# A recurrent attention kernel whose banks for projections, gate inputs and output quarters are dealt out anew, with VectorE's additions in another order

## The chip, the cores and the metric

The kernel runs on one core of one Trainium2 chip. The metric is the device time of one execution in microseconds (us). TensorE (PE) multiplies, VectorE (DVE) and ScalarE (ACT) read and write the accumulator memory PSUM and the on-chip memory SBUF, GpSimd (POOL) works on SBUF alone, and SyncE (SP) issues the DMAs. Every engine works through a list of its own in order, and the engines wait for each other through semaphores. PSUM has eight banks here, numbered 0 to 7; each holds 512 fp32 values in each of the 128 partitions.

## The reference, cut to what matters

For an input of 4 batches, 512 tokens and 256 features:

```python
xn = layernorm(x)
s  = attention(xn)               # below, 16 key heads, two value heads for each
g  = silu(feed_forward(xn))      # weights are looked up in a table of 16 values
out = x + s * g

# attention, for each head
q, k, v = silu(causal_conv(xn @ W_qkv, 4 taps))
z = xn @ W_z
T = inverse(I + strictly_lower(beta * k @ k.T * decay))      # chunks of 64 tokens
v_c, k_cumdecay = T @ (v * beta), T @ (k * beta * exp(g))
for each chunk:                                              # 8 chunks, in sequence
    v_new = v_c - k_cumdecay @ state
    o     = (q * exp(g)) @ state + (q @ k.T * decay) @ v_new
    state = state * exp(g_last) + (k * exp(g_last - g)).T @ v_new
s += (norm_w * rmsnorm(o) * silu(z)) @ W_out
```

## The kernel before

The work is done in 32 rounds. A round is one key head (`R.h`) with two of the four batches (`R.par`), and holds two value heads of 512 tokens in 8 chunks. A round has three stages, and each engine's part of them is written out by hand:

- `begin`: products of keys with keys and queries, and transposes. VectorE then inverts the 16x16 diagonal blocks alone (`small_blocks`, ends with L1175) while TensorE projects the first half of the **next** round's q, k, v (`proj` 0 to 3) and adds the **previous** round's output quarters 0 and 1 (`outputs`, kind `out`, L680).
- `invert`: two levels (16 to 32, 32 to 64) complete the inverse. A level is `products` first (L482, L484, banks 2 and 3), ScalarE's copy (`first_products`, L872), `products` second (L487, L489), and VectorE's predicated copy into the inverse (`second_products`, L1200). Between these TensorE does what the tables at the top of the program name for each place (`beside`): the rest of the projections (`PROJ_AT`, L425), output quarters of the previous round (`OUT_AT`), and inputs of the gate (`Z_AT`, `zproj`, L452). VectorE fills its time with the convolution of the next round's projections: for each of four kinds (key, query, two values) ScalarE makes tap 0 (`tap0`, L772), VectorE adds taps 1 to 3 out of the banks (`taps`, L1024), ScalarE applies silu (`silu`, L780). VectorE also scales the previous round's last quarter of the attention (`gated` 3, L1285), out of the bank into which TensorE has turned it (`turn_back` 3, kind `ot3`, L667), and adds the four output quarters (128 tokens of two batches each) to the sum `acc` (L1294).
- `keys_through` (L580: the keys go through the inverse; kind `kcd`, four groups in banks 4, 5, 6, 7, two for each batch), ScalarE's copies of them (L918), and then `recur`, the chain over the 8 chunks. It opens with half of the last gate input (z3), and `old_part` (L588), which needs banks 4 and 5 empty again; VectorE's L1245 follows it.

Order on ScalarE behind the second level: silu of value 0, gate 0, silu of value 1 (`silu` 3, waits for the last of all the taps), gates 1 and 2 (`gate`, L812, each reads one z bank), the copies of `kcd`, gate 3.

What ties the work together is `bank_uses`: a list for each round of (use, bank). Every use of a bank waits until the one before it in the same bank has been read. `wait_open` and `wait_full` look the numbers up, `full[n]` counts what TensorE has filled in bank n and `read[n]` what has been read from it. `keys_through` waits for both banks of a batch before its first product. `both` names the PSUM tensor that starts at an even bank, because a kind's two batches are read as one pair of banks.

Of the kernel before, what the change touches and what calls it, by code (L numbers as in the profile page):

```python
# [42 lines left out]
IN_LEVELS = 3  # L43
OUT_LAST = {(5, 1): (3,)}
PROJ_FIRST = (0, 1, 2, 3)
PROJ_AT = {(4, 1): (4, 5), (5, 1): (6, 7)}
OUT_AT = {(4, 0): (1,), (5, 0): (2,), (5, 1): (3,)}
Z_AT = {(5, 1): (0, 1, 2)}
GATE_UP_AT = {(4, 0): ((0, 0),), (4, 1): ((0, 1),), (5, 0): ((1, 0), (1, 1)), (5, 1): ((2, 0), (2, 1))}
PROJ = [("proj", i) for i in range(8)]  # L50
# [7 lines left out]
def bank_uses(it):  # L58

    first, nxt = it == 0, it < ROUNDS - 1  # L60
    begin = (spread([("kkq", i) for i in range(2)], (4, 5)) + spread([("kt", i) for i in range(2)], (6, 7))
             + spread([("vt", i) for i in range(4)], (1, 4, 5, 7)))
    ahead = spread(PROJ, (0, 1, 6, 7)) if nxt else []
    outs = [] if first else spread([("out", 0), ("out", 1), ("out", 2), ("ot3", 0), ("out", 3)], (5, 4, 5, 4, 4) if nxt else (5, 4, 7, 4, 5))
    levels = []
    for lv in LEVELS:
        levels += spread([("p1", (lv, b)) for b in range(BB)], (2, 3)) + spread([("p2", (lv, b)) for b in range(BB)], (2, 3))
    small = spread([("z", i) for i in range(4)], (5, 0, 1, 0) if nxt else (0, 1, 0, 0)) + (spread(N2, (0, 1)) if nxt else [])
    keys = spread([("kcd", i) for i in range(4)], (4, 5, 6, 7))
    steps = spread([("vn", n) for n in range(NC * BB)], (4, 5)) + spread([("sp", c) for c in range(NC - 1)], (6,))  # L70
    turns = spread([("o", i) for i in range(4)], (2, 3)) + spread([("ot", i) for i in range(3 if nxt else 4)], (1,))
    end = [] if nxt else spread([("end", i) for i in range(4)], (0, 2))
    return begin + outs + ahead + levels + small + keys + steps + turns + end


def all_places():
# [61 lines left out]
def build(nc, x, consts, resets_in, wqkvz, wba, convw, dtb, alog, normw, wout, lut, idx, out):  # L138
    g_dram = nc.dram_tensor("g_scratch", (B, HV, S), F32, kind="Internal").ap()
    fw_dram = nc.dram_tensor("fw_scratch", (HQK, 2, P, SLICE), F32, kind="Internal").ap()  # L140
    with ExitStack() as ctx:
# [78 lines left out]
        ps_p2 = ctx.enter_context(nc.psum_tensor("ps_p2", [P, BB, 512], F32))  # L220
        ps_state = ctx.enter_context(nc.psum_tensor("ps_state", [P, RATIO, 512], F32))
        ps = [t[:, n, :] for t in (ps_two, ps_p1, ps_p2, ps_state) for n in range(2)]
        both = {0: ps_two, 6: ps_state}
        G = ps_p1[:, 0, 0:BASE * (BASE + 1)]
        full = [sem(f"full{i}") for i in range(8)]
        read = [sem(f"read{i}") for i in range(8)]
# [154 lines left out]
        def _(pe):  # L381
# [134 lines left out]
            def invert(R):  # L516

                if R.nxt:
                    for i in PROJ_FIRST:
                        proj(R, i)  # L520
                if R.before() is not None:
                    for t in range(1 if R.nxt else 3):
                        outputs(R, "out", R.before(), t)
                    if R.nxt:
                        outputs(R, "out", R.before(), 1, (0,))
                for n, lv in enumerate(LEVELS):
                    pe.wait_ge(s["xs"], R.at(1 + 2 * n, 0, 4))
# [15 lines left out]

            def beside(R, lv, half):

                if R.before() is not None and (lv, half) == (5, 1):
                    turn_back(R.before(), 3)
                if R.nxt:
                    for i in PROJ_AT.get((lv, half), ()):
                        proj(R, i)  # L550
                else:
                    for f, j in GATE_UP_AT[lv, half]:
                        if f == 0 and j == 0:
                            pe.wait_ge(s["ld_fw"], 16)
                        if f == 1 and j == 0:
                            wait_read(pe, R, "out", 2)
                        if f >= 2 and j == 0:
                            pe.wait_ge(s["ff_h"], f - 1)
                        gate_up(f, f, 0, j, AHEAD[f])
                if R.before() is not None:  # L560
                    for t in (OUT_AT if R.nxt else OUT_LAST).get((lv, half), ()):
                        outputs(R, "out", R.before(), t, (1,) if t == 1 else (0, 1))
# [181 lines left out]
        def _(act):  # L744
# [94 lines left out]
            def invert(R):  # L839
                if R.nxt:  # L840
                    tap0(R, 0)
                if R.nxt:
                    tap0(R, 1)
                small_x(R)
                swap(R, 0)
                first_products(R, 4)
                if R.nxt:
                    silu(R, 0)
                swap(R, 1)
                if R.nxt:  # L850
                    tap0(R, 2)
                else:
                    gated_unit(0, 0, AHEAD[0])
                first_products(R, 5)
                if R.nxt:
                    silu(R, 1)
# [94 lines left out]
        def _(dve):  # L951
# [249 lines left out]

            def invert(R):
                of = R.before()
                if R.nxt:
                    taps(R, 0, (1, 2, 3))
                if of is not None:
                    for t in range(1 if R.nxt else 3):
                        outputs(R, "out", of, t)
                second_products(R, 4, 2)
                turn()  # L1210
                if R.nxt:
                    taps(R, 1, (1, 2, 3))
                else:
                    hidden(0, 0, AHEAD[0])
                    hidden(1, 1, AHEAD[1])
                if R.nxt and of is not None:
                    outputs(R, "out", of, 1)
                second_products(R, 5, 4)
                if of is not None:
                    gated(of, 3)  # L1220
                if R.nxt and of is not None:
                    outputs(R, "out", of, 2)
                if R.nxt:
                    taps(R, 2, (1, 2, 3))
                else:
                    hidden(2, 2, AHEAD[2])
                if of is not None:
                    outputs(R, "out", of, 3)
                if R.nxt:
                    taps(R, 3, (1, 2, 3))  # L1230

            def second_products(R, lv, n):

# [278 lines left out]
```

## Time and profile before

| what | us |
|---|---|
| median of 3 runs (2178.72 to 2179.42) | 2178.77 |
| the profiled execution | 2178.21 |
| its span, first to last instruction | 2176.4 |
| from one round to the next in mid-run | 61.3 |
| TensorE busy | 2070.3 |
| GpSimd busy | 1670.5 |
| VectorE busy | 1597.4 |
| ScalarE busy | 1192.7 |

Busy shares are means over stages that differ. For this change only the middle of a round is needed: from the end of `small_blocks` to the first chunk of `recur`. The timeline of each engine shows it: an instruction's start, its length, and in square brackets how long the engine had stood idle before it and who released it.

### The profile page before, as it was taken

How to read it: one execution, taken by the hardware profiler on the slowest of the kernel's cores; microseconds unless marked ns; L12 is line 12 of the kernel's file. 1: busy time of each engine (PE TensorE's matmuls, PEld its weight loads, DVE VectorE, ACT ScalarE, POOL GpSimd, SP SyncE). 2: the span in 40 equal slices, each digit the busy share in tenths (PEclk: the TensorE clock that was granted, in tenths of full speed). 3: DMA queues.
4: the chain of work that ended last, by engine and by line, in shares of the span. 5: the costliest groups of instructions: out<-in, count | busy, mean ns of one | idle time of the engine just before them, and what ended most of it. 6: DMA issues, size and time to landing. Idle time of an engine off the chain costs nothing.

```text
span 2176.4 us, 75165 instructions
## 1 busy us (share of the span) xinstructions
PE 2070.3 (95%) x31952; PEld 1578.1 (73%) x31952; DVE 1597.4 (73%) x3083; ACT 1192.7 (55%) x2757; POOL 1670.5 (77%) x1774
## 2 busy tenths in 40 slices
PE   3799999999999999999999999999999999999998
PEld 2677777777777777777777777777777777776644
DVE  5777777778777777778777777778777777776322
ACT  3565556655665556655665556655665556654211
POOL 2788888888888888888888888888888888888200
PEclk9899999999999999999999999999999999999999
DMA  2211101111121101121121102111121102111100
GB/s 87 58 41 39 48 17 41 39 48 34 36 48 39 47 16 44 39 49 34 36 48 39 47 14 46 39 48 34 36 48 39 48 11 48 39 39 45 45 15 20
DMA packets 57485, 86.31 MB, mean 40 GB/s; under 512 B 7488, under 2 KB 30144, under 8 KB 57152
## 3 DMA queue, kind: packets, MB, share of 16 engines
q1 hardware_dynamic: 57152, 81.50, 15.2%
q8 instruction: 254, 4.16, 0.8%
q14 instruction: 79, 0.65, 0.1%
HBM read 76.92 MB, written 4.55 MB: 37 GB/s over the span
## 4 chain that ended last, share of the span: by engine, by line
PE 49%; DVE 33%; ACT 9%; issue 6%; POOL 2%; DMA 0%; DVEq 0%; POOLq 0%; SPq 0%; ACTq 0%
DVE cacc L1024 11%; PE ps_two L452 8%; PE ps_state L425 5%; PE ps_p L615 4%; DVE terms L1126 3%; PE ps_p L501 3%; ACT qg L799 3%; PE ps_state L639 3%; PE ps_p L680 3%; PE ps_p L623 3%; PE ps_p L588 3%; PE ps_p L452 2%; PE ps_p L739 2%; ACT L790 2%; PE ps_two L539 2%
## 5 line engine op out<-in xcount | busy, mean ns | idle before, releaser
L1411 POOL TENSOR_SCALAR Kg<-idx_s,lutb 128x134 f32<-128x134 int32 x480 | 356.3, 745 | 27.1
L1372 POOL TENSOR_TENSOR Sd<-St,el 128x512 f32<-128x512 f32 x192 | 201.3, 1048 | 196.9 <-DVEq L1266 196.9
L1245 DVE TENSOR_SCALAR Vn<-ps_p,bR 128x128 f32<-128x128 f32 x512 | 165.9, 349 | 189.8 <-PE ps_p L588 114.1
L425 PE MATMUL ps_two<-xnT,w_qkv 128*128 128x256 f32 x1024 | 235.7, 383 | 17.7 <-DVEq L1029 17.7
L1024 DVE SCALAR_TENSOR_TENSOR cacc<-ps_state,cw,cacc 128x1022 f32<-128x1022 f32 (+2 forms) x192 | 244.2, 1272 | 7.9 <-ACT cacc L772 3.1
L1024 DVE SCALAR_TENSOR_TENSOR cacc<-ps_two,cw,cacc 128x1022 f32<-128x1022 f32 (+2 forms) x192 | 244.8, 1275 | 5.3 <-DVE cacc L1024 0.5
L680 PE MATMUL ps_p<-w_o,hT 128*128 128x256 f32 x1000 | 242.4, 386 | 1.6 <-ACT V L835 1.6
L425 PE MATMUL ps_state<-xnT,w_qkv 128*128 128x256 f32 x1024 | 234.0, 382 | 5.9 <-DVEq L1029 5.9
L425 PEld LDWEIGHTS ps_two<-xnT,w_qkv 128*128 128x128 f32 x1024 | 190.3, 191 | 44.3 <-DVEq L1029 21.0
L425 PEld LDWEIGHTS ps_state<-xnT,w_qkv 128*128 128x128 f32 x1024 | 193.7, 192 | 32.3 <-DVEq L1029 6.3
L927 ACT ACTIVATE P<-ps_p 128x128 f32<-128x128 f32 x256 | 67.2, 277 | 267.7 <-PE ps_p L593 267.7
L680 PEld LDWEIGHTS ps_p<-w_o,hT 128*128 128x128 f32 x1000 | 185.2, 190 | 27.6 <-issue 2.8
L1264 DVE TENSOR_TENSOR St<-Sd,ps_state 128x256 f32<-128x256 f32 x384 | 144.4, 417 | 68.8 <-PE ps_state L639 39.0
L452 PE MATMUL ps_two<-xnT,w_z 128*128 128x512 f32 x388 | 188.9, 610 | 0.2
L1383 POOL TENSOR_TENSOR qg<-qg,kq 128x512 f32<-128x512 f32 x128 | 166.5, 1324 | 17.6 <-DVE blocks L1097 17.6
L615 PE MATMUL ps_p<-St,Kg 128*64 128x128 f32 x1792 | 163.3, 294 | 6.3 <-DVE St L1264 6.1
L588 PE MATMUL ps_p<-V,XW 64*64 64x128 f32 x2048 | 159.6, 271 | 0.0
L593 PE MATMUL ps_p<-Vn,A 64*64 64x128 f32 x2048 | 155.9, 270 | 3.5
L1417 POOL TENSOR_TENSOR Kg<-Kg 128x536 f32<-128x536 f32 (+2 forms) x128 | 142.4, 1112 | 10.2
L639 PE MATMUL ps_state<-Vn,Kd 64*64 64x128 f32 x3584 | 149.6, 282 | 0.1
L772 ACT ACTIVATE cacc<-ps_state,cw 128x1024 f32<-128x1024 f32 x64 | 71.2, 1113 | 135.9 <-PE ps_state L425 101.0
L588 PEld LDWEIGHTS ps_p<-V,XW 64*64 64x64 f32 x2048 | 120.9, 133 | 24.7 <-ACT Kg L918 23.5
(192 smaller groups left out, 5014.4 us busy)
## 6 DMA issues: line engine op xcount, KB each, us to landing
qg<-g_scratch SPq DMA_DIRECT2D x64, 512.0 KB, 6.2
g_st<-g_scratch SPq DMA_DIRECT2D x64, 256.0 KB, 8.6
w_qkv<-in_wqkvz SPq DMA_DIRECT2D x16, 512.0 KB, 3.8
w_z<-in_wqkvz SPq DMA_DIRECT2D x16, 256.0 KB, 3.3
w_o<-in_wout SPq DMA_DIRECT2D x16, 256.0 KB, 2.9
idx_s<-in_idx SPq DMA_DIRECT2D x32, 67.0 KB, 1.9
fw_scratch<-looked_up SPq DMA_DIRECT2D x32, 67.0 KB, 2.7
Kg<-in_x SPq DMA_DIRECT2D x2, 1024.0 KB, 5.7
```

What stands on the lines that cost most here:

```text
L425: m = pe.matmul(bank[:, t0:t0 + S // 2], w_qkv[:, k, kind * P:(kind + 1) * P], rows, start=(k == 0), stop=(k == KD - 1))
L452: m = pe.matmul(bank[:, :], w_z[:, k, a * P:(a + 1) * P], xnT[:, k, cols(R.par, b)], start=(k == 0), stop=(k == KD - 1))
L588: return pe.matmul(bank[r, 0:P], X[r, b, c, :], V[r, b, c, :], start=True, stop=(c == 0), skip_group_check=True)
L593: return pe.matmul(o_bank[turned[a], o0:o0 + P], A[r, b, c, :], Vn[r, c % 2, b, :], start=(c == 0 and b == 0), stop=True, skip_group_check ...
L615: m = pe.matmul(olds[b][0][r, 0:P], Kg[:, b, c, r], St[:, cur, a, b, :], start=False, stop=True, skip_group_check=True)
L639: m = pe.matmul(ps[6 + a][half, b * P:(b + 1) * P], Kd[r, b, c, half], Vn[r, cur, b, :], start=True, stop=True)
L680: m = pe.matmul(bank[:, b * D:(b + 1) * D], hT[:, t, a, 1 - b, :], w_o[:, a, :], start=(a == 0), stop=(a == RATIO - 1))
L1024: dve.scalar_tensor_tensor(dst, both[n][:, :, 0:S - t], cw[:, kind, 3 - t:4 - t], dst, ALU.mult, ALU.add).then_inc(s["taps"], 1)
L1245: dve.tensor_scalar(Vn[:, cur, b], bank[:, 0:P], bR[:, R.par, b, c:c + 1], None, ALU.mult).then_inc(done, 1)
L1372: pool.tensor_tensor(Sd[:, :, :, :], St[:, c % 2, :, :, :], el[:, R.par, :, :, c].unsqueeze(3).broadcast_to([P, BB, RATIO, P]), ALU.mult). ...
L1383: m = pool.tensor_tensor(dst, dst, kq[:, :, 1, b, :], ALU.mult)
L1411: m = pool.tensor_scalar(slots[k], idx_s[:, :], float(k), lutb[:, k:k + 1], ALU.is_equal, ALU.mult)
```

## The change

The table of banks and the two orders (TensorE's and VectorE's) are rewritten for the rounds that have a next one (31 of 32; the last round keeps its order and banks). In words:

- Banks. The next round's projections 4 to 7 move from banks 0, 1, 6, 7 to 4, 5, 0, 1. Output quarter 2 moves from bank 5 to 6, the turned quarter `ot3` and output quarter 3 from bank 4 to 7. The gate inputs z0, z1, z2 move from 5, 0, 1 to 4, 5, 2.
- TensorE. Output quarter 1 stands whole behind the first products of level 4; half of it stood ahead of them. Output quarter 2 leaves its place between the products of level 5; projection 6 takes it. At the end of the levels comes projection 7, then `ot3`, then quarters 2 and 3.
- VectorE. Output 0 is added ahead of the first tap of kind 0, output 1 behind this tap; tap 1 of kind 2 goes ahead of `gated` 3, and taps 2 and 3 behind it; then outputs 2 and 3 together, then the taps of kind 3.
- ScalarE. Tap 0 of kind 2 goes behind the copy of level 5's first products; it stood ahead.

```diff
-PROJ_AT = {(4, 1): (4, 5), (5, 1): (6, 7)}
-OUT_AT = {(4, 0): (1,), (5, 0): (2,), (5, 1): (3,)}
+PROJ_AT = {(4, 1): (4, 5), (5, 0): (6,), (5, 1): (7,)}
+OUT_AT = {(4, 0): (1,), (5, 1): (2, 3)}
...
-    ahead = spread(PROJ, (0, 1, 6, 7)) if nxt else []
+    ahead = spread(PROJ, (0, 1, 6, 7, 4, 5, 0, 1)) if nxt else []
...
-    small = spread([("z", i) for i in range(4)], (5, 0, 1, 0) if nxt else (0, 1, 0, 0)) + (spread(N2, (0, 1)) if nxt else [])
+    small = spread([("z", i) for i in range(4)], (4, 5, 2, 0) if nxt else (0, 1, 0, 0)) + (spread(N2, (0, 1)) if nxt else [])
...
-                    if R.nxt:
-                        outputs(R, "out", R.before(), 1, (0,))
```

TensorE, end of the levels up to `recur`, in a round of mid-run (`ps_p2` is banks 4 and 5, `ps_state` 6 and 7, `ps_two` 0 and 1, `ps_p1` 2 and 3; `waits read5` is the wait until bank 5 has been read). Before:

```order
L452 MATMUL ps_p2<-xnT,w_z 128x512 [waits read5,ld_wz]
L452 MATMUL ps_p2<-xnT,w_z 128x512
L452 MATMUL ps_two<-xnT,w_z 128x512 [waits read0]
L452 MATMUL ps_two<-xnT,w_z 128x512
L452 MATMUL ps_two<-xnT,w_z 128x512 [waits read1]
L452 MATMUL ps_two<-xnT,w_z 128x512
L580 MATMUL ps_p2<-XW,Kg 64x64 [waits read4,read5,kg_c,xs]
L580 MATMUL ps_p2<-XW,Kg 64x64 x31
L580 MATMUL ps_state<-XW,Kg 64x64 [waits read6,read7,kg_c,xs]
```

The same place now:

```order
L453 MATMUL ps_p2<-xnT,w_z 128x512 [waits read4,ld_wz]
L453 MATMUL ps_p2<-xnT,w_z 128x512
L453 MATMUL ps_p2<-xnT,w_z 128x512 [waits read5]
L453 MATMUL ps_p2<-xnT,w_z 128x512
L453 MATMUL ps_p1<-xnT,w_z 128x512 [waits read2]
L453 MATMUL ps_p1<-xnT,w_z 128x512
L582 MATMUL ps_p2<-XW,Kg 64x64 [waits read4,read5,kg_c,xs]
L582 MATMUL ps_p2<-XW,Kg 64x64 x31
L582 MATMUL ps_state<-XW,Kg 64x64 [waits read6,read7,kg_c,xs]
```

The second gate input (z1) stood in bank 0 and stands in bank 5 now, the bank that the key products behind it write.

VectorE, from the end of `small_blocks` (XW) through the first level. Before:

```order
L1175 TENSOR_SCALAR XW<-terms,cst 128x16x16
L1024 SCALAR_TENSOR_TENSOR cacc<-ps_two,cw,cacc 128x2x511 [waits tap0]
L1024 SCALAR_TENSOR_TENSOR cacc<-ps_two,cw,cacc 128x2x510 [waits taps]
L1024 SCALAR_TENSOR_TENSOR cacc<-ps_two,cw,cacc 128x2x509 [waits taps]
L1294 TENSOR_TENSOR acc<-acc,ps_p2 128x2x256 [waits taps,full5]
L1198 MEMSET carry 128x1 [waits full3,full2]
L1200 COPY_PREDICATED XW<-cst,ps_p1 128x32x16
```

Now (`waits full4` is the wait until TensorE has filled bank 4):

```order
L1176 TENSOR_SCALAR XW<-terms,cst 128x16x16
L1298 TENSOR_TENSOR acc<-acc,ps_p2 128x2x256 [waits full5]
L1025 SCALAR_TENSOR_TENSOR cacc<-ps_two,cw,cacc 128x2x511 [waits tap0]
L1298 TENSOR_TENSOR acc<-acc,ps_p2 128x2x256 [waits full4]
L1025 SCALAR_TENSOR_TENSOR cacc<-ps_two,cw,cacc 128x2x510 [waits taps]
L1025 SCALAR_TENSOR_TENSOR cacc<-ps_two,cw,cacc 128x2x509 [waits taps]
L1199 MEMSET carry 128x1 [waits taps,full3,full2]
L1201 COPY_PREDICATED XW<-cst,ps_p1 128x32x16
```

Output 1 stands behind the first tap, and what follows it on the engine waits with it.

TensorE around the first level, with the 32x32 and 64x32 products of the level left out. Before:

```order
L680 MATMUL ps_p2<-w_o,hT 128x256 [waits read4,normed_o]
L680 MATMUL ps_p2<-w_o,hT 128x256
...
L680 MATMUL ps_p2<-w_o,hT 128x256 x2
...
L425 MATMUL ps_two<-xnT,w_qkv 128x256 [waits read0]
L425 MATMUL ps_two<-xnT,w_qkv 128x256 x3
L425 MATMUL ps_two<-xnT,w_qkv 128x256 [waits read1]
L425 MATMUL ps_two<-xnT,w_qkv 128x256 x3
```

Now:

```order
L682 MATMUL ps_p2<-w_o,hT 128x256 [waits read4,normed_o]
L682 MATMUL ps_p2<-w_o,hT 128x256 x3
...
L426 MATMUL ps_p2<-xnT,w_qkv 128x256 [waits read4]
L426 MATMUL ps_p2<-xnT,w_qkv 128x256 x3
L426 MATMUL ps_p2<-xnT,w_qkv 128x256 [waits read5]
L426 MATMUL ps_p2<-xnT,w_qkv 128x256 x3
```

Two matmuls of quarter 1 stood ahead of the first products and two behind; all four stand behind now. Projection 4 waited for bank 0, and waits for bank 4.

## Rows read from the trace of the kernel before

**Rows 1.** The page: busy time of the engines, and the chain that ended last.

```profile
PE 2070.3 (95%) x31952; PEld 1578.1 (73%) x31952; DVE 1597.4 (73%) x3083; ACT 1192.7 (55%) x2757; POOL 1670.5 (77%) x1774
PE 49%; DVE 33%; ACT 9%; issue 6%; POOL 2%; DMA 0%; DVEq 0%; POOLq 0%; SPq 0%; ACTq 0%
```

**Rows 2.** Timeline of VectorE, one round: start us, length us, engine, line, operation.

```profile
887.62 0.65 DVE L1175 TENSOR_SCALAR XW<-terms,cst 128x256 f32<-128x256 f32 x2
888.19 3.89 DVE L1024 SCALAR_TENSOR_TENSOR cacc<-ps_two,cw,cacc 128x1022 f32<-128x1022 f32 x3
892.32 0.69 DVE L1294 TENSOR_TENSOR acc<-acc,ps_p 128x512 f32<-128x512 f32 x1 [0.25 <-DVE cacc L1024]
892.93 0.74 DVE L1200 COPY_PREDICATED XW<-cst,ps_p 128x512 f32<-128x512 int32 x1
...
893.91 0.71 DVE L1190 STREAM_TRANSPOSE XW<-XW 128x512 f32<-128x512 f32 x1 [0.24 <-DVE XW L1200]
894.55 3.87 DVE L1024 SCALAR_TENSOR_TENSOR cacc<-ps_state,cw,cacc 128x1022 f32<-128x1022 f32 x3
...
900.36 0.75 DVE L1285 SCALAR_TENSOR_TENSOR hT<-ps_p,gpar,z 128x512 f32<-128x512 f32 x1 [0.24 <-PE ps_p L667]
901.26 0.69 DVE L1294 TENSOR_TENSOR acc<-acc,ps_p 128x512 f32<-128x512 f32 x1
...
906.62 3.90 DVE L1024 SCALAR_TENSOR_TENSOR cacc<-ps_state,cw,cacc 128x1022 f32<-128x1022 f32 x3
913.97 0.61 DVE L1245 TENSOR_SCALAR Vn<-ps_p,bR 128x128 f32<-128x128 f32 x2 [3.45 <-PE ps_p L588]
...
948.89 0.65 DVE L1175 TENSOR_SCALAR XW<-terms,cst 128x256 f32<-128x256 f32 x2
```

**Rows 3.** Timeline of TensorE in the same round.

```profile
885.40 2.75 PE L680 MATMUL ps_p<-w_o,hT 128*128 128x256 f32 x12
888.32 0.24 PE L482 MATMUL ps_p<-XW,U 64*64 64x32 f32 x1 [0.17 <-DVE XW L1175]
...
889.38 1.13 PE L680 MATMUL ps_p<-w_o,hT 128*128 128x256 f32 x4
...
892.19 3.72 PE L425 MATMUL ps_two<-xnT,w_qkv 128*128 128x256 f32 x16 [0.59 <-DVEq L1029]
...
896.52 1.99 PE L680 MATMUL ps_p<-w_o,hT 128*128 128x256 f32 x8
...
899.50 0.63 PE L667 MATMUL ps_p<-cst,on 128*128 128x128 f32 x4 [0.30 <-DVE acc L1294]
...
906.86 3.60 PE L452 MATMUL ps_two<-xnT,w_z 128*128 128x512 f32 x8
910.39 1.16 PE L580 MATMUL ps_p<-XW,Kg 64*64 64x64 f32 x64
...
912.43 1.12 PE L452 MATMUL ps_two<-xnT,w_z 128*128 128x512 f32 x2
913.48 0.66 PE L588 MATMUL ps_p<-V,XW 64*64 64x128 f32 x8
```

**Rows 4.** Timeline of ScalarE in the same round.

```profile
892.11 1.06 ACT L780 ACTIVATE kq<-cacc 128x1024 f32<-128x1024 f32 x1 [1.91 <-DVE cacc L1024]
...
910.55 1.06 ACT L780 ACTIVATE vs<-cacc 128x1024 f32<-128x1024 f32 x1 [2.89 <-DVE cacc L1024]
911.52 1.06 ACT L812 ACTIVATE z<-ps_two 128x512 f32<-128x512 f32 x2
912.47 1.08 ACT L918 ACTIVATE Kg<-ps_p 128x512 f32<-128x512 f32 x2
```

**Rows 5.** Waits of the whole run: engine and line, releaser, us in total, times, longest.

```profile
PEld ps_p L588 <- ACT Kg L918: 23.5, 31, 0.8
```

**Rows 6.** Timeline of TensorE in the first round.

```profile
92.31 0.31 PE L482 MATMUL ps_p<-XW,U 64*64 64x32 f32 x1 [3.57 <-DVE XW L1175]
```

**Rows 7.** Window of it: length, busy PE, PEld, DVE, ACT, POOL, then PEclk.

```profile
92.30:94.30 2.00, 1.93 (x64) 1.80 (x64) 1.96 (x2) 1.17 (x2) 1.77 (x4) 0.50 0.04 8
```

More of the change, by code:

```diff
@@ L62, in bank_uses @@
              + spread([("vt", i) for i in range(4)], (1, 4, 5, 7)))
-    ahead = spread(PROJ, (0, 1, 6, 7)) if nxt else []
-    outs = [] if first else spread([("out", 0), ("out", 1), ("out", 2), ("ot3", 0), ("out", 3)], (5, 4, 5, 4, 4) if nxt else (5, 4, 7, 4, 5))
+    ahead = spread(PROJ, (0, 1, 6, 7, 4, 5, 0, 1)) if nxt else []
+    outs = [] if first else spread([("out", 0), ("out", 1)], (5, 4))
+    late = [] if first else spread([("out", 2), ("ot3", 0), ("out", 3)], (6, 7, 7) if nxt else (7, 4, 5))
     levels = []
@@ L72, in bank_uses @@
     end = [] if nxt else spread([("end", i) for i in range(4)], (0, 2))
-    return begin + outs + ahead + levels + small + keys + steps + turns + end
+    return begin + outs + ahead + late + levels + small + keys + steps + turns + end
 def all_places():
@@ L222, in build @@
         ps = [t[:, n, :] for t in (ps_two, ps_p1, ps_p2, ps_state) for n in range(2)]
-        both = {0: ps_two, 6: ps_state}
+        both = {0: ps_two, 4: ps_p2, 6: ps_state}
         G = ps_p1[:, 0, 0:BASE * (BASE + 1)]
@@ L544, in beside @@
             def beside(R, lv, half):
-                if R.before() is not None and (lv, half) == (5, 1):
+                turn = R.before() is not None and (lv, half) == (5, 1)
+                if turn and not R.nxt:
                     turn_back(R.before(), 3)
@@ L550, in beside @@
                         proj(R, i)
+                    if turn:
+                        turn_back(R.before(), 3)
                 else:
@@ L561, in beside @@
                     for t in (OUT_AT if R.nxt else OUT_LAST).get((lv, half), ()):
-                        outputs(R, "out", R.before(), t, (1,) if t == 1 else (0, 1))
+                        outputs(R, "out", R.before(), t)
                 for i in Z_AT.get((lv, half), ()):
@@ L849, in invert @@
                 swap(R, 1)
-                if R.nxt:
-                    tap0(R, 2)
-                else:
+                if not R.nxt:
                     gated_unit(0, 0, AHEAD[0])
@@ L855, in invert @@
                 if R.nxt:
+                    tap0(R, 2)
                     silu(R, 1)
@@ L1203, in invert @@
                 of = R.before()
-                if R.nxt:
-                    taps(R, 0, (1, 2, 3))
-                if of is not None:
-                    for t in range(1 if R.nxt else 3):
-                        outputs(R, "out", of, t)
+                if not R.nxt:
+                    for t in range(3):
+                        outputs(R, "out", of, t)
+                    second_products(R, 4, 2)
+                    turn()
+                    hidden(0, 0, AHEAD[0])
+                    hidden(1, 1, AHEAD[1])
+                    second_products(R, 5, 4)
+                    gated(of, 3)
+                    hidden(2, 2, AHEAD[2])
+                    outputs(R, "out", of, 3)
+                    return
+                if of is not None:
+                    outputs(R, "out", of, 0)
+                taps(R, 0, (1,))
+                if of is not None:
+                    outputs(R, "out", of, 1)
+                taps(R, 0, (2, 3))
                 second_products(R, 4, 2)
                 turn()
[L1211 to L1217, printed above, removed]
+                taps(R, 1, (1, 2, 3))
                 second_products(R, 5, 4)
+                taps(R, 2, (1,))
                 if of is not None:
                     gated(of, 3)
-                if R.nxt and of is not None:
+                taps(R, 2, (2, 3))
+                if of is not None:
                     outputs(R, "out", of, 2)
[L1223 to L1227, printed above, removed]
                     outputs(R, "out", of, 3)
-                if R.nxt:
-                    taps(R, 3, (1, 2, 3))
+                taps(R, 3, (1, 2, 3))
             def second_products(R, lv, n):
```

## The prediction

> **What bounds the kernel now.** I read the chain of waits first, then the timelines of the three engines over one round of mid-run, and last the table of waits. The page names TensorE, 95% busy, and a chain that is half TensorE and a third VectorE [rows 1]: in some stretch of each round VectorE is what comes last. Rounds follow each other every 61.27 us (L1175 at 887.62 and at 948.89 [rows 2]), and their rows repeat within some hundredths, so one round, times 31, is the sum.
>
> The round's middle begins when VectorE ends the small inverse (L1175, 887.62 + 0.65 = 888.27). TensorE starts the first products at 888.32, behind an idle time of 0.17 only [rows 3]. VectorE then has no gap above 0.25 us until its last tap ends at 906.62 + 3.90 = 910.52 [rows 2]. TensorE is just as full: one stop of 0.59 before projection 4 (banks 0 and 1, which the taps of kind 0 read), one of 0.30 before the turned quarter, and then no gap through the gate inputs, the key products (L580, 910.39) and half of z3, up to `old_part` (L588, 913.48) [rows 3]. ScalarE joins at the end: silu of the last value at 910.55, 0.03 behind the last tap, gates 1 and 2 at 911.52, the first two key copies at 912.47, ended at 913.55 [rows 4]. `old_part` starts together with their end, and the weight loads of L588 waited for the copies in 31 rounds, 0.76 us each [rows 5]. So two chains meet at 913.5: TensorE's own queue, and VectorE's last tap, silu, gates, copies. Nothing shortens a round there unless both get shorter, and either can lengthen it alone. VectorE's first V_new (L1245, 913.97) follows.
>
> **The change part by part.** Before the end of the small inverse TensorE loses half an output quarter, 12 records of L680 becoming 8. It was waiting there for VectorE anyhow (0.17), and the first products still wait for L1175: worth nothing.
>
> *Term A, VectorE's wait for output 1.* VectorE now does output 0 (start to start 892.93 - 892.32 = 0.61) and one tap (3.89 / 3 = 1.30) from 888.19 on, and would be ready for output 1 at 888.19 + 0.61 + 1.30 = 890.10. TensorE reaches the quarter only behind the first products, at 889.38, and a whole quarter takes 1.99 (L680 x8), not the 1.13 of a half [rows 3]: it ends at 891.37, and I put VectorE's start at 891.44, a release later. That is 1.34 us of idle time on a full engine. The additions and taps are otherwise the same instructions, and their 0.24 and 0.25 stops behind a tap or a predicated copy are as many as before; one start-to-start distance shrinks by about 0.1 because an output no longer stands ahead of the second predicated copy. Followed through by these lengths: taps of kind 0 end at 894.65 (before 892.08), the second products of level 4 are long there, the turn starts 895.87 (before 893.91), taps of kind 1 end 900.40, and the last tap of kind 3 ends at 911.77. **A = 911.77 - 910.52 = 1.25 us** a round.
>
> What else VectorE needs on this way should be there in time. The second products of level 5 stand behind projection 6 now (half of 3.72), so TensorE ends them at about 899.9; VectorE asks at 900.6. The turned quarter stands behind projection 7 and ends at about 902.3; VectorE asks at 902.9. ScalarE's silu of the key moves with the taps from 892.11 to 894.67, and its copy of level 5's first products ends near 898.7, under projection 6, which covers TensorE until 899.2. These covers are 0.5 to 0.7 us thick; if one fails, VectorE ends by that much later.
>
> *Term B, the key products wait for gate 1.* z1 is in bank 5 now, and the key products of batch 0 wait for banks 4 and 5 before their first matmul. Bank 5 is read by gate 1, and gate 1 stands on ScalarE behind the silu that waits for the last tap. Before, gate 1 started 911.52 - 910.52 = 1.00 behind the last tap, and one of the two takes about 0.59 (two in 1.06) [rows 4]. With 0.06 for the release TensorE can start 1.65 behind the last tap. Before it started 0.13 **ahead** of it (910.39 against 910.52 [rows 3]), because bank 5 held z0, whose gate runs much earlier, and bank 4 output 3. **B = 1.65 + 0.13 = 1.78 us.** Behind the waiting product stand all the key products, z3 and `old_part`, with nothing in between that could be pulled ahead. VectorE is idle by then (3.45 before L1245), and ScalarE has only gate 2 to do: no work hides the wait.
>
> *Term C, what TensorE gets back.* Banks 6 and 7 are empty earlier (output 2 and 3 instead of projections 6 and 7), but TensorE gets to them behind the products that wait. The 0.59 and 0.30 stops go, and the time is spent in front of the later wait: the gate inputs, started about 906.5 when the taps of kind 2 have left bank 4, end at about 911.7, 1.7 us before gate 1 is through. Behind the key products the two halves of the end chain no longer meet: the copies have 2.04 us of key products and half of z3 to run under. The distance from L580 to L588 was 3.09 (910.39 to 913.48); half of z3 alone is 0.88 of it by the pace of the other gate inputs (3.60 for four matmuls less a tail), against the 1.05 it stood for. **C = -0.15 us.**
>
> Sum of a round: 1.25 + 1.78 - 0.15 = 2.88 us. The first round has no previous outputs, but has the same gate 1 in bank 5, and the last has no next round and keeps its order; with 31 rounds the sum is 31 x 2.88 = 89 us. The profiled execution, 2178.21 (span 2176.4 and 1.8 around it), becomes 2267.5; the median of the runs is 0.56 above the profiled one: 2268, and I round the unknown release times up to **2269 us**.
>
> The bounds: A is nothing at least, if VectorE takes up the wait elsewhere, and at most 1.34 + 0.7 with one failed cover. B lies between 1.6 (the gate's start and length, no release) and 1.9. C lies between 0 and -0.76, the whole wait of L588's weights for the copies [rows 5]. A round costs 0.8 to 3.9 with all ends on one side, and 2.3 to 3.5 where they are not: 2250 to 2287.
>
> A page speaks for this change. The Trainium skill, Perfetto Trace Analysis, section Optimizing Tensor Performance, says that independent matmul groups should rotate through different banks, so that one group's evacuation overlaps the next group's matmuls. By that alone the key products gain, since two of their four banks come free earlier; it gives the second rival below. The trace agrees on the evacuations (TensorE runs on through z0 to z2 while gate 0 reads), but what decides here is which instruction empties the bank and what stands ahead of it on its engine.
>
> **The rivals.** *Only B.* VectorE's wait for output 1 costs nothing in the end, since the last tap also waits for things that come at their old time. The round costs 1.78 - 0.15 = 1.63, 31 of them 51 us: 2229. Against it: VectorE's rows show no slack between L1175 and the last tap that could take 1.3 us up.
>
> *TensorE's queue decides: faster.* If the key products find bank 5 empty when TensorE comes to them, as now, because gate 1 does get ahead of the last tap, TensorE's queue alone counts. It saves the stops of 0.59 and 0.30 and pays 1.99 - 1.13 = 0.86 for the half quarter that stood under a wait: together -0.03, and up to -0.15 more at z3. 31 rounds give -1 to -6 us, 2173 to 2178. It decides if the gate is through by 910.4; for it speaks that TensorE is the fuller engine of the page [rows 1], against it that ScalarE works in order, that the order puts gate 1 behind the silu of the last value, and that this silu began 0.03 behind the last tap [rows 4].
>
> *The change does not do what it says*: moved work fills the same waits and the round stays within 0.1 us. It would need both of the above to cancel: 2175 to 2182.
>
> *The clock falls.* TensorE's stop before the key products grows to some 1.7 us in every round. In the first round it stood for 3.57 us before the first products [rows 6], and these ran at a granted clock of 0.50, its 1.2 GHz level, and took 1.93 for the 64 matmuls [rows 7] that take 889.38 - 888.32 = 1.06 in mid-run: 1.8 times as long. If 1.7 us were enough, the 2.9 us from the key products to `old_part` would take 2.3 more, 71 us in all: 2340. The trace has stops of 0.59 in every round at the full clock and none of 1.7, so it does not exclude this. The Trainium skill, TensorE: Matmul & The Clock Gate, says that the gate follows how busy TensorE has recently been; the first round agrees, and whether 1.7 us is enough no row shows.
>
> **How the numbers follow.** Forecast (A, B and C as above) 0.80, 2269, its own bounds 2250 to 2287. Only B 0.10, 2229. One cover failed and more, 0.03, up to 2300. Clock 0.02, 2340. TensorE's queue decides 0.03, 2176. No change 0.02. The range 2250 to 2287 holds the first and leaves out the rest. A measurement of this kernel tells about 0.2% (4.4 us) from no change: faster by more 0.02, within 0.03, slower by more 0.95.
>
> **What would show it.** In the profile after: idle time of 1.2 to 1.4 us before VectorE's first L1298 output 1, released by TensorE's L682 (A); 31 stops of about 1.7 us before L582, released by ScalarE's gate L814, and the weight loads of L590 no longer waiting for the copies (B, C); the last tap ending some 23.5 us behind L1176 (22.25 before); rounds 64.1 us apart; PEclk at 1.00. The prediction is wrong if L582 starts before the last tap ends, if VectorE's last tap is not later than before, or if a cover fails and VectorE shows a new wait for full3 or full7.

## The result

| | before | after |
|---|---|---|
| median, us | 2179.10 (2178.72 to 2180.78, 4 runs) | 2302.64 (2300.26 to 2304.75, 4 runs) |
| the profiled execution, us | 2178.21 | 2302.11 |
| its span, us | 2176.4 | 2300.3 |
| an ordinary round, us | 61.26 | 64.40 |
| TensorE busy, us | 2070.3 | 2091.2 |
| VectorE busy, us | 1597.4 | 1591.7 |

The ratio is 1.0567, 95% interval 1.0551 to 1.0583. The sign and the two mechanisms of the forecast hold, and the time lies 16 us above the range, which ended at 2287.

The page of after, answering [rows 1], has TensorE's share of the last chain down from 49% to 36% and VectorE's up from 33% to 43%:

```profile
PE 2091.2 (91%) x31952; PEld 1578.3 (69%) x31952; DVE 1591.7 (69%) x3083; ACT 1194.9 (52%) x2757; POOL 1669.8 (73%) x1774
DVE 43%; PE 36%; ACT 11%; issue 7%; POOL 2%; DVEq 0%; DMA 0%; POOLq 0%; SPq 0%; ACTq 0%
```

VectorE in an ordinary round of after (start, length, engine, line, operation, then the idle time before it and who ended it), answering [rows 2]:

```profile
943.19 0.65 DVE L1176 TENSOR_SCALAR XW<-terms,cst 128x256 f32<-128x256 f32 x2
943.76 0.67 DVE L1298 TENSOR_TENSOR acc<-acc,ps_p 128x512 f32<-128x512 f32 x1
944.35 1.27 DVE L1025 SCALAR_TENSOR_TENSOR cacc<-ps_two,cw,cacc 128x1022 f32<-128x1022 f32 x1
946.99 0.69 DVE L1298 TENSOR_TENSOR acc<-acc,ps_p 128x512 f32<-128x512 f32 x1 [1.37 <-PE ps_p L682]
...
963.48 3.90 DVE L1025 SCALAR_TENSOR_TENSOR cacc<-ps_two,cw,cacc 128x1022 f32<-128x1022 f32 x3
972.68 0.61 DVE L1249 TENSOR_SCALAR Vn<-ps_p,bR 128x128 f32<-128x128 f32 x2 [5.29 <-PE ps_p L590]
```

The small inverse ends at 943.84. The last tap ends at 967.38, 23.54 later, and V_new starts at 28.84. In [rows 2] these distances were 910.52 - 888.27 = 22.25 and 913.97 - 888.27 = 25.70. VectorE waits 1.37 us for output 1 and 5.29 before V_new (3.45 before).

TensorE and ScalarE in the same round, answering [rows 3] and [rows 4]:

```profile
944.96 1.99 PE L682 MATMUL ps_p<-w_o,hT 128*128 128x256 f32 x8
...
962.24 5.39 PE L453 MATMUL ps_p<-xnT,w_z 128*128 128x512 f32 x12 [0.78 <-DVEq L1030]
969.11 1.16 PE L582 MATMUL ps_p<-XW,Kg 64*64 64x64 f32 x64 [1.48 <-ACT z L814]
970.06 1.15 PE L582 MATMUL ps_state<-XW,Kg 64*64 64x64 f32 x64
971.14 1.12 PE L453 MATMUL ps_two<-xnT,w_z 128*128 128x512 f32 x2
972.19 0.65 PE L590 MATMUL ps_p<-V,XW 64*64 64x128 f32 x8
```

```profile
967.42 1.06 ACT L782 ACTIVATE vs<-cacc 128x1024 f32<-128x1024 f32 x1 [2.59 <-DVE cacc L1025]
968.38 1.07 ACT L814 ACTIVATE z<-ps_p 128x512 f32<-128x512 f32 x2
```

The whole of output quarter 1 ends at 946.95, and VectorE takes output 1 at 946.99. The key products start at 969.11, 1.73 behind the last tap (25.27 behind the small inverse; 22.12 before), when the first of the two gates is through. `old_part` follows 3.08 later. Over the whole run (engine and line, releaser, us in total, times, longest):

```profile
DVE acc L1298 <- PE ps_p L682: 46.4, 33, 3.9
PE ps_p L582 <- ACT z L814: 44.7, 30, 1.8
PE ps_state L582 <- issue: 14.0, 8, 2.4
```

The third line has no counterpart before. An ordinary round is one of the length that most rounds share. Ordinary rounds are 64.40 apart, 3.14 longer, and 31 x 3.14 = 97.3 us. The other 26 us lie elsewhere. In ten rounds (counted from 0: 0, 5, 6, 10, 11, 16, 21, 22, 27, 28) TensorE stops once more in the middle of the key products or just behind them, 0.5 to 2.4 us, with "issue" as releaser: it waited for nothing that the profile shows. Round 11:

```profile
838.62 1.16 PE L582 MATMUL ps_p<-XW,Kg 64*64 64x64 f32 x64 [1.48 <-ACT z L814]
839.58 1.14 PE L582 MATMUL ps_state<-XW,Kg 64*64 64x64 f32 x60
842.06 0.33 PE L582 MATMUL ps_state<-XW,Kg 64*64 64x64 f32 x4 [1.35 <-issue]
```

The stops sum to 15.5 us. The nine such rounds behind round 0 are together 20.8 us longer than nine ordinary ones, partly because the clock also fell in rounds 5 and 10. Round 0 is 66.74 long (60.29 before), 3.3 beyond the 3.14; the last round is 1.4 longer. 97.3 + 20.8 + 3.3 + 1.4 = 122.8, of 123.9 between the spans.

### The profile page after: what moved, and what is told of

Read it like the earlier page. It is cut to its first block, busy times and chain, and to the rows that moved or that the text cites. A ratio compares the mean times of both kernels' runs of the same rounds, so it can differ in the third digit from the quotient of the medians.

```text
span 2300.3 us, 75165 instructions
## 1 busy us (share of the span) xinstructions
PE 2091.2 (91%) x31952; PEld 1578.3 (69%) x31952; DVE 1591.7 (69%) x3083; ACT 1194.9 (52%) x2757; POOL 1669.8 (73%) x1774
## 3 DMA queue, kind: packets, MB, share of 16 engines
q8 instruction: 254, 4.16, 0.8%
## 4 chain that ended last, share of the span: by engine, by line
DVE 43%; PE 36%; ACT 11%; issue 7%; POOL 2%; DVEq 0%; DMA 0%; POOLq 0%; SPq 0%; ACTq 0%
DVE cacc L1025 18%; PE ps_p L617 4%; PE ps_two L453 3%; DVE terms L1127 3%; PE ps_p L682 3%; PE ps_p L502 3%; ACT qg L801 3%; DVE acc L1298 3%; PE ps_state L641 3%; PE ps_p L590 2%; PE ps_p L625 2%; PE ps_p L741 2%; DVE XW L1201 2%; ACT L792 2%; PE ps_two L538 2%
## 5 line engine op out<-in xcount | busy, mean ns | idle before, releaser
L426 PE MATMUL ps_two<-xnT,w_qkv 128*128 128x256 f32 x1024 | 243.2, 385 | 0.0
L453 PE MATMUL ps_p<-xnT,w_z 128*128 128x512 f32 x372 | 170.0, 607 | 26.2 <-DVEq L1030 26.2
L590 PE MATMUL ps_p<-V,XW 64*64 64x128 f32 x2048 | 160.6, 272 | 1.5 <-issue 1.5
L782 ACT ACTIVATE vs<-cacc 128x1024 f32<-128x1024 f32 x64 | 67.5, 1057 | 166.5 <-DVE cacc L1025 166.5
L782 ACT ACTIVATE kq<-cacc 128x1024 f32<-128x1024 f32 x64 | 67.6, 1057 | 164.5 <-DVE cacc L1025 164.5
L453 PEld LDWEIGHTS ps_p<-xnT,w_z 128*128 128x128 f32 x372 | 69.2, 193 | 113.8 <-issue 113.8
L590 PEld LDWEIGHTS ps_p<-V,XW 64*64 64x64 f32 x2048 | 121.8, 134 | 26.5 <-issue 26.5
L1402 POOL TENSOR_TENSOR rr<-ss,cst 128x4 f32<-128x4 f32 x128 | 129.8, 1014 | 10.0
L625 PE MATMUL ps_p<-St,qg 128*64 128x128 f32 x1792 | 135.9, 273 | 0.0
L641 PEld LDWEIGHTS ps_state<-Vn,Kd 64*64 64x64 f32 x3584 | 95.5, 132 | 58.8 <-issue 36.0
```

The costliest lines, as they stand in the source:

```text
L426: m = pe.matmul(bank[:, t0:t0 + S // 2], w_qkv[:, k, kind * P:(kind + 1) * P], rows, start=(k == 0), stop=(k == KD - 1))
L453: m = pe.matmul(bank[:, :], w_z[:, k, a * P:(a + 1) * P], xnT[:, k, cols(R.par, b)], start=(k == 0), stop=(k == KD - 1))
L590: return pe.matmul(bank[r, 0:P], X[r, b, c, :], V[r, b, c, :], start=True, stop=(c == 0), skip_group_check=True)
L625: pe.matmul(o_bank[turned[a], o0:o0 + P], qg[:, R.par, a, b, c * C:(c + 1) * C], St[:, cur, a, b, :], start=(cur == 0 and b == 0), stop=False,
L641: m = pe.matmul(ps[6 + a][half, b * P:(b + 1) * P], Kd[r, b, c, half], Vn[r, cur, b, :], start=True, stop=True)
```

## The experiments

Four kernels take the two terms and the extra stops apart, and three more (e5, e6, e7) test what sets the pace of an ordinary round. Offsets below are from the end of the small inverse of that kernel, in ordinary rounds; that of the key products is their first weight load's, 0.03 ahead of the first matmul. Extra stops are TensorE's "issue" stops in or right behind the key products.

| kernel | median, us | last tap | key products | V_new | round | extra stops, us |
|---|---|---|---|---|---|---|
| before | 2179 | 22.25 | 22.11 | 25.69 | 61.26 | 0 |
| after | 2302.6 | 23.54 | 25.23 | 28.84 | 64.40 | 15.5 |
| e1 | 2234.1 | 23.54 | 23.71 | 27.29 | 62.88 | 0 |
| e2 | 2239.6 | 23.54 | 23.71 | 27.29 | 62.87 | 5.5 |
| e3 | 2262.5 | 22.26 | 23.95 | 27.55 | 63.12 | 17.1 |
| e4 | 2310.1 | 23.54 | 25.23 | 28.83 | 64.41 | 20.8 |
| e5 | 2206.8 | 22.68 | 22.84 | 26.44 | 62.01 | 0 |
| e6 | 2159.8 | 22.11 | 21.33 | 25.06 | 60.65 | 0 |
| e7 | 2178.9 | 22.26 | 22.11 | 25.70 | 61.28 | 0 |

**e1: the change with z1 out of bank 5.** Are the 1.5 us before the key products, and the extra stops with them, owed to bank 5?

```diff
-    small = spread([("z", i) for i in range(4)], (4, 5, 2, 0) if nxt else (0, 1, 0, 0)) + (spread(N2, (0, 1)) if nxt else [])
+    small = spread([("z", i) for i in range(4)], (4, 2, 3, 0) if nxt else (0, 1, 0, 0)) + (spread(N2, (0, 1)) if nxt else [])
```

> The changed kernel with one edit in the table of banks: the gate inputs z1 and z2 in banks 2 and 3 in place of 5 and 2, so that the key products no longer share a bank with z1. Theory (gate 1 holds bank 5 until behind the last tap, and TensorE, stopped in front of a dense run of small matmuls, runs out of fetched instructions in some rounds): the stop of 1.48 us before the key products goes, they start 23.8 us behind the small inverse (25.2 now), VectorE's first V_new stands at 27.1 (28.8 now, 25.7 before), no round has a stop of issue on TensorE in or behind the key products, and the time is 2178.8 + 31 x 1.4 = 2222 us, 2215 to 2232. Rival (VectorE's later last tap alone decides, the gate only fills time that is lost anyway): V_new stays at 28.8 or above 28.3 and the time stays above 2285.

Measured: 2234.09 (2230.84 to 2235.25), ratio 1.0252 (1.0236 to 1.0267). The time is 2 us above the range I gave. The last tap stays at 23.54, the wait for the gate is gone, and so are all extra stops:

```profile
931.51 5.39 PE L453 MATMUL ps_p<-xnT,w_z 128*128 128x512 f32 x12 [0.77 <-DVEq L1030]
936.83 1.16 PE L582 MATMUL ps_p<-XW,Kg 64*64 64x64 f32 x64
937.82 1.13 PE L582 MATMUL ps_state<-XW,Kg 64*64 64x64 f32 x64
```

The gate inputs now set the start of the key products. They wait for VectorE's taps of kind 2, which read bank 4, and end at 23.7. So z1's place in bank 5 costs 68.5 us of the 123 (z2 goes to bank 3 to make room): 31 x 1.52 = 47 by the ordinary rounds, the rest by what came with the wait. The remaining 1.6 a round belongs to the rest of the change: the two new orders and the other banks, z0's in bank 4 among them. e5 below takes 0.87 of it back.

**e2: the change with gate 1 ahead of the silu of value 1.** Bank and wait stay, and the releaser comes earlier.

```diff
+                    gate(R, 1)
                     silu(R, 3)
...
-                gate(R, 1)
```

> The changed kernel, all banks as it has them, with ScalarE's gate 1 moved ahead of the silu of the last value. The same question from the other side: bank 5 is emptied while VectorE is still in its last taps. Theory: as the kernel with z1 in bank 2, key products at 23.8 us, V_new at 27.1, no stops of issue, 2222 us (2215 to 2232). Rival: 2285 or more, since the silu stands 0.6 us further back on ScalarE only if the gate is not ready, and VectorE's end is unchanged.

Measured: 2239.57 (2238.29 to 2242.48), ratio 1.0277 (1.0260 to 1.0294). I had expected no extra stops and at most 2232. Ordinary rounds are those of e1, but rounds 0, 5, 10, 11, 16, 21, 22 and 27 stop again, shorter, 0.42 to 0.90 us. Round 10 of e2:

```profile
752.25 1.16 PE L582 MATMUL ps_p<-XW,Kg 64*64 64x64 f32 x64
753.23 0.77 PE L582 MATMUL ps_state<-XW,Kg 64*64 64x64 f32 x37
754.70 0.68 PE L582 MATMUL ps_state<-XW,Kg 64*64 64x64 f32 x27 [0.70 <-issue]
```

TensorE shows no wait before the products here, and yet the extra stop is there, of 0.70. What changed is when their wait is released: gate 1, at 750.64 and 0.60 long, ends 1.0 us ahead of them; in the change it ends 0.14 us ahead.

**e3: the kernel before with z1 in bank 5 alone.**

```diff
-    small = spread([("z", i) for i in range(4)], (5, 0, 1, 0) if nxt else (0, 1, 0, 0)) + (spread(N2, (0, 1)) if nxt else [])
+    small = spread([("z", i) for i in range(4)], (0, 5, 1, 0) if nxt else (0, 1, 0, 0)) + (spread(N2, (0, 1)) if nxt else [])
```

> The kernel before with one edit: z0 in bank 0 and z1 in bank 5 (they stood in 5 and 0). Nothing else of the change is in it. Theory: the key products wait for gate 1 as in the changed kernel and start 1.65 us behind the last tap (23.9 us behind the small inverse, 22.1 now), V_new at 27.3 (25.7 now), 31 x 1.6 = 50 us, and 15 to 25 us of instruction stops and slow clock in a third of the rounds on top: 2240 to 2255. Rival on the second half (the stops of issue come from another part of the change, the banks of the projections or the load of weights): V_new at 27.3 in every round, no stops of issue, 2226 to 2234. Rival on the first (the whole loss is in VectorE's order): 2178 to 2185.

Measured: 2262.49 (2261.82 to 2267.91), ratio 1.039 (1.0374 to 1.0405). z0 goes to bank 0 in exchange. Nothing else of the change is in it: the last tap stays at 22.26, and the round is 1.86 longer.

```profile
951.39 1.16 PE L580 MATMUL ps_p<-XW,Kg 64*64 64x64 f32 x64 [0.88 <-ACT z L812]
```

Its time is 7 us above the range I gave: a round costs 1.86 and not 1.6, which makes 58 us, and what comes on top is 25.5, at the upper end of the 15 to 25 I gave it. The extra stops come with the wait: 17.1 us in the same ten rounds. In round 10 it breaks off behind the same 37th matmul of the second half as the change and e2.

**e4: the change, shifted.** In the change, e2 and e3 round 10 breaks behind matmul 64 + 37. Count all of TensorE's instructions in the trace together, from 0: matmuls, weight loads, and its 1,105 semaphore and drain instructions, which the timeline leaves out. The key products of round 10 begin at a number that leaves 245 over 256. Behind 101 matmuls with their loads, and the two semaphore instructions between the two halves, the next is 245 + 2 x 101 + 2 = 449, which is 193 over 256. Round 11 begins at 199 and breaks behind 64 + 60 (199 + 2 x 124 + 2 = 449), round 0 at 193 behind 127 (449). In all 28 extra stops of the change, e2 and e3, those just behind the products too, the last instruction to go through stands 192 over a multiple of 256. Counted by matmuls and loads alone the stops share no such place. If it is a matter of place in the program, small repeated matmuls in the prologue must move it to other rounds (64 matmuls by the page, with their loads 128 instructions; they only repeat work).

```diff
+                    if R.head and i == 0:
+                        for _ in range(32):
+                            pe.matmul(bank[0:C, 0:WIDE], flat(sqk)[:, 0:C], ones[:, 0:WIDE], start=True, stop=True)
```

> The changed kernel with 32 more small matmuls in the prologue (each is repeated work, overwritten before it is read): 128 more records of TensorE ahead of every round, half of a block of 256 instructions in which they are fetched. Theory (a round stops when a block's border lies in the first 70 records behind the wait): the rounds with a stop of issue of 0.5 to 2.5 us, numbered from 0, are 5, 6, 10, 11, 16, 21, 22, 27, 28 in the changed kernel and become about 2, 7, 8, 13, 14, 19, 24, 25, 30; their number and the time stay, 2296 to 2310. Rival (the stops come with the weight load that SyncE issues behind the last tap of every second round, or with something else that has its place in the round's number): the stops stay in the same rounds. In every second round they cannot be, since 5, 11, 21, 27 and 6, 10, 16, 22 are both odd and even.

Measured: 2310.06 (2307.38 to 2312.98), ratio 1.0603 (1.0587 to 1.0619), at the upper end of the range. The extra stops are now in rounds 2, 7, 8, 13, 14, 18, 19, 24, 25 and 30. All ten stand behind number 192 over a multiple of 256 again. Nine of the rounds were named beforehand, from products that begin at 185 or more; round 18 was not: they begin at 5 there, and the border falls 187 instructions in. In the change's round 4 they begin at 9, the border falls 183 in, and there is no stop. Ordinary rounds are unchanged at 64.41. Round 2, whose products begin at 229 now, breaks behind matmul 64 + 45 (229 + 2 x 109 + 2 = 449):

```profile
246.75 1.16 PE L585 MATMUL ps_p<-XW,Kg 64*64 64x64 f32 x64 [1.48 <-ACT z L817]
247.70 0.90 PE L585 MATMUL ps_state<-XW,Kg 64*64 64x64 f32 x45
250.92 0.56 PE L585 MATMUL ps_state<-XW,Kg 64*64 64x64 f32 x19 [2.32 <-issue]
```

What lies behind it shows in the page's DMA queues. Two queues are of the kind "instruction". One of them, q8, moves 254 packets of 16 KB in the whole run, and TensorE has 65,009 instructions in the trace: one packet for every 256. The trace's view of the DMA in a short window (busy share in 40 slices, then the queue) finds the packet of round 11. In the kernel before, from 785.00 to 789.00, the products start at 787.86 and the packet stands in the 15th slice, at 786.4, 1.4 us ahead of them:

```profile
DMA  0000000000000070000000000000000000000000
q8 instruction: 1, 0.02, 1.9%
```

In the change, from 838.60 to 841.00 (products from 838.62), it stands in the 19th slice, at 839.7, 1.1 us **behind** their start:

```profile
DMA  0000000000000000009000000000000000000000
q8 instruction: 1, 0.02, 2.4%
```

TensorE goes on at 842.06. The reading that fits the change and e1 to e4: the stream is brought in by blocks of 256, and it is brought as TensorE's front end (the part that takes in its instructions) gets on. While the first key product waits for the gate, the front end stands there, and nothing more is fetched. Once released, the 256 matmuls and loads of the key products start within 1.9 us, and in the change, e3 and e4 the next block is not there yet wherever the border lies behind 187 or more of them, and in some rounds with the border just behind them all. In the change's rounds 5 to 28 TensorE went on 3.4 to 4.3 us behind the first key product, so a border that it reaches 1.5 to 2 us behind it costs 1.3 to 2.4.

That the stops sit at a fixed place in the stream (e4), need the wait (e1) and shrink when the gate ends earlier (e2) is shown by the runs. That TensorE stands there for the packet is shown by every packet's start and length in the nine traces. Number the packets of q8 from 0 and give packet n the block that begins at number 256 x (n + 1) + 193. Round 11's packet is number 90: it takes 0.93 us from 839.73, and TensorE goes on 1.4 us behind its end. In all 38 extra stops, 0.4 to 2.8 us long, TensorE goes on 1.2 to 1.6 us behind the end of that packet; and at none of the 2,277 borders in the nine traces does TensorE start the next block sooner than 1.2 us behind its packet's end. In all 38 the packet starts 1.0 to 2.4 us behind the end of gate 1. In the kernel before, a packet starts when TensorE has 87 to 297 instructions left to its border; in the change it is down to none in rounds 10 and 16.

**e5: e1 with half of output quarter 1 ahead of the first products again.** This tests term A alone.

```diff
                     for t in range(1 if R.nxt else 3):
                         outputs(R, "out", R.before(), t)
+                    if R.nxt:
+                        outputs(R, "out", R.before(), 1, (0,))
...
-                        outputs(R, "out", R.before(), t)
+                        outputs(R, "out", R.before(), t, (1,) if t == 1 else (0, 1))
```

> The change with z0, z1, z2 in banks 4, 2, 3 (as in e1) and, besides, half of output quarter 1 back ahead of the first products of level 4, as before. My theory (term A is TensorE's whole quarter behind the first products): VectorE's stop before output 1 falls from 1.37 to about 0.45 us, the last tap ends 22.65 us behind the small inverse (23.54 in e1), the key products start 22.8, a round takes about 62.0 (62.88 in e1), and the run about 2206 us (2200 to 2213). Rival (only B costs; the last tap also waits for things that come at their old time): last tap and rounds as in e1, 2234.

Measured: 2206.79 (2204.99 to 2208.71), ratio 1.0122 (1.0107 to 1.0138), 27 us less than e1. VectorE's stop falls from 1.37 to 0.50, and everything behind it moves by the same 0.86:

```profile
905.04 0.69 DVE L1300 TENSOR_TENSOR acc<-acc,ps_p 128x512 f32<-128x512 f32 x1 [0.50 <-PE ps_p L684]
```

The rival that the last tap waits for things at their old time is out: the 0.86 that VectorE gets back ahead of the last tap comes off the round whole (62.88 to 62.01).

**e7: the kernel before with gates 1 and 2 ahead of the silu of value 1.** The prediction let two chains meet at `old_part`: TensorE's queue, and gates and key copies. Here the second gets shorter.

```diff
+                    gate(R, 1)
+                    gate(R, 2)
                     silu(R, 3)
...
-                gate(R, 1)
...
-                gate(R, 2)
```

> The kernel before with one edit: ScalarE's gates 1 and 2 go ahead of the silu of value 1, so that the key copies follow this silu directly. My theory: the copies no longer stand behind the gates, but TensorE's queue then sets the start of old_part, 0.1 to 0.2 us earlier; 2174 us (2170 to 2179). Rival (the key copies alone set it): 0.76 a round, 2155.

Measured: 2178.94 (2177.07 to 2179.64), ratio 0.9993 (0.9985 to 1.0002): no difference, where I had expected 0.1 to 0.2 us a round. `old_part` still starts at 25.21. The idle time of its weight loads [rows 5] is the same amount under another name:

```profile
PEld ps_p L588 <- issue: 24.3, 32, 0.8
```

The copies were never what it waited for. PEld's idle time there is only the matmuls of z3 going on; the first loads run right behind them, whoever came last.

**e6: a version of the kernel before that shortens both.** Gates 1 and 2 go ahead of the silu of value 1, output quarter 2 ahead of projection 4, projection 5 between the products of level 5, and VectorE's order is moved to suit.

```diff
-PROJ_AT = {(4, 1): (4, 5), (5, 1): (6, 7)}
-OUT_AT = {(4, 0): (1,), (5, 0): (2,), (5, 1): (3,)}
+PROJ_AT = {(4, 1): (4,), (5, 0): (5,), (5, 1): (6, 7)}
+OUT_AT = {(4, 0): (1,), (4, 1): (2,), (5, 1): (3,)}
...
+                    gate(R, 1)
+                    gate(R, 2)
                     silu(R, 3)
...
+                if R.nxt:
+                    taps(R, 2, (1,))
```

> The kernel before with ScalarE's gates 1 and 2 ahead of the silu of value 1, output quarter 2 ahead of projection 4, projection 5 between the products of level 5, and VectorE's order moved to suit. My theory (in the kernel before, old_part waits for both TensorE's own queue and the key copies behind gates 1 and 2): both get shorter, L588 starts about 0.8 us earlier in a round, 2155 us (2150 to 2172). Rival one (VectorE's last tap is bound by the full engine and silu and copies follow it whatever the gates do): 2174. Rival two (the instruction fetch stops that e3 and the change showed come here too): above 2180.

Measured: 2159.76 (2158.24 to 2160.69), ratio 0.9905 (0.9892 to 0.9919): 0.95% faster than before. The key products start at 21.33, now ahead of the last tap at 22.11, and ScalarE's silu has no gate between itself and the copies:

```profile
900.51 0.60 ACT L818 ACTIVATE z<-ps_two 128x512 f32<-128x512 f32 x1 [1.12 <-PE ps_two L452]
901.23 1.06 ACT L786 ACTIVATE vs<-cacc 128x1024 f32<-128x1024 f32 x1
902.19 1.06 ACT L925 ACTIVATE Kg<-ps_p 128x512 f32<-128x512 f32 x2
```

The round is 0.62 shorter, not the 0.8 I expected: from the first key product's start to the last one's it is 2.04 and not 1.89, and from them to `old_part` it is 3.25 and not 3.10. In this version no extra stop appears. As the gates alone brought nothing (e7), the gain needs TensorE's shorter queue; whether that alone would do, with the gates in their old place, was not run.

## Why the prediction was right about two waits and wrong about the time

**Term A, right.** 1.25 forecast, 23.54 - 22.25 = 1.29 measured; the stop before output 1 is 1.37 (1.34 forecast). e5 shows that this stop makes it. The covers held: no new wait for the turned quarter or for the second level.

**Term B, right.** The first key matmul starts 1.73 behind the last tap in most rounds (1.65 forecast), and was 0.13 ahead of it: 1.86 against 1.78. e3 has it alone, 1.86 a round with nothing else changed.

**Term C, wrong and small.** I forecast -0.15, because the key copies would no longer hold up `old_part`. The distance from L582 to L590 is 3.08, against 3.09 before: nothing came back. The step that failed took the idle time of the weight loads [rows 5] for a wait on the path. Matmuls ran all through it, and e7 removes the releaser named there without moving the round. Half of z3 takes 1.05 from its start to L590's with the copies out of the way too (971.14 to 972.19; 912.43 to 913.48 before), so the 0.88 that I took from the pace of the other gate inputs was not to be had here; their row, which I read as four matmuls, has eight. A row of the weight loads is a wait only where the row of the matmuls behind it shows one too. Without C the sum is 3.03, and 3.14 was measured.

**The step that made the time wrong: "with 31 rounds the sum is 31 x 2.88".** It took every round for the one I read. With A, B and C as measured (1.29 + 1.86 - 0.01) it gives 31 x 3.14 = 97, and 2276, inside the range. The other 26 us are in rounds that are not like the others: ten with a block border behind the new wait (20.8 for the nine behind round 0), and round 0. In the prediction's own terms, B was the wait alone, and what the wait does to the fetch of TensorE's instructions, and with it to the clock in two rounds, was put at nothing. The trace of before held the pieces, 254 instruction packets and the densest stretch of small matmuls right behind the place where I put a wait, but none of its rows showed a stop. I had put a gate's wait at its plain length.

**Round 0, wrong.** I took the first round as any other. It has no output quarters and shows no wait for the gate before the key products, but its z0 stands in bank 4 now, and waits for the taps of kind 2:

```profile
110.87 2.04 PE L453 MATMUL ps_p<-xnT,w_z 128*128 128x512 f32 x2 [3.34 <-DVEq L1030]
```

Within this stop of 3.34, at 110.01, the granted clock fell to 0.50, the 1.2 GHz level, for 6.8 us. Before, z0 had bank 5 and no stop. e1, which has the same z0, has the same slow stretch and a round 0 of 65.35, so most of the cost lies there and not in bank 5. In e4 the stop is 3.35, the slow stretch 3.4, and round 0 takes 64.19.

**The clock, a rival that came true in two rounds.** I asked whether stops of 1.7 us before the key products let the clock fall. Alone they do not; this window (length, busy PE, PEld, DVE, ACT, POOL, then PEclk) holds a stop of 1.48 and the products behind it:

```profile
969.00:973.00 4.00, 3.89 (x139) 2.93 (x140) 0.32 (x2) 2.52 (x5) 0.38 (x1) 1.00 0.01 4
```

In round 10 a second stop, of 2.41, followed the first of 1.48 within two microseconds, and then it fell:

```profile
773.00:776.00 3.00, 1.89 (x31) 0.96 (x33) 0.00 (x0) 1.08 (x2) 0.00 (x0) 0.94 0.00 0
776.00:780.00 4.00, 4.00 (x44) 2.00 (x44) 1.01 (x3) 0.94 (x2) 0.00 (x0) 0.62 0.02 4
```

In round 5 it fell behind 1.48 and 1.68, and in rounds 16 and 22, with 2.06 and 2.18 as second stops, it did not. The Trainium skill, TensorE: Matmul & The Clock Gate, says in Part 1 that the gate follows how busy the engine has recently been; the fall behind two stops and not behind one agrees, and these rows do not say from where on it falls.

**The rule on banks.** The Trainium skill, Perfetto Trace Analysis, section Optimizing Tensor Performance, would have independent groups rotate through the banks. The kernel does so before and after. What cost 68.5 us is which engine's instruction empties the bank that is next, and what that instruction stands behind.

## What to carry to other kernels

Before giving a bank to a new tenant, name the instruction that will empty it and everything queued ahead of that instruction on its engine; here a gate behind a silu behind VectorE's last tap made one bank number cost 1.5 us a round. A wait of more than a microsecond put in front of a dense run of small matmuls costs more than its length, in the rounds where the instruction stream needs its next block in that run. Sum over the rounds, not one round times their number, and look for "issue" stops that recur at a fixed place in the count of the engine's instructions, semaphore instructions included. And an idle time of PEld with matmuls running through it is no wait.

## What the runs showed of the hardware that I had not expected

- TensorE's instructions arrive during the run: 254 packets, 4.16 MB, 256 instructions to a packet. The Trainium skill, Trainium Architecture — The Big Picture, section The software stack, tells of the streams as brought into the engines' memory when the program is loaded; the trace shows a packet in transfer at 839.7 us of the span, so for a stream of this size that is not the whole of it.
- Behind a wait of about 1.5 us, TensorE went on 3.4 to 3.6 us after the release in the odd ones of the stopping rounds, and 3.9 to 4.3 in the even ones. The packet's own transfer is no longer there (0.9 to 1.0 us in the even rounds, 0.9 to 1.3 in the odd ones); it starts later, 1.7 to 1.9 us behind the first key product against 1.0 to 1.1. In the even rounds the next head's weights (`w_qkv`, 512 KB) are in transfer just then: in the 3.1 us from 769.90, round 10, the DMA engines were busy 0.51 of the time, and in those from 838.60, round 11, 0.02. That the packet starts late because of that load is likely, and no run separated it.
- In e2 no wait is to be seen before the key products on TensorE's timeline, and 5.5 us of the 15.5 us of extra stops remain. A wait that is over before the engine gets there can still cost.
- What stays open: what passes between the release and the packet's start (1.0 to 1.9 us from the first key product in the change's rounds 5 to 28), and in the 1.2 to 1.6 us between the packet's end and TensorE going on.
